# The last edge sum in 16-bit terms: rows of 384 bfloat16 values in place of 128 float32 values

## The reference, cut to what matters

```
h = maximum(layernorm(x), 0.0)
x = x + segment_sum(take(h, dst), src, num_segments=6250)
```

## Time and profile before

| | |
|---|---|
| median of 3 runs | 11695.7 us |
| profiled execution | 11690.42 us |
| its span | 11688.7 us |
| from the end of layer 3's sum to the first gather of `sum_phase` | 9243 to 9330 us |
| gathers of `sum_phase`, 1616 | 9330.3 to 11658.3 us |
| `final_phase` and the stores | 11671.4 to 11688.7 us |

### The profile page before, as it was taken

How to read it: one execution, slowest core, us unless ns; L and a number is a source line. 1 busy time by engine, 2 the same in 40 slices (tenths; PEclk the granted TensorE clock), 3 DMA queues, 4 the chain that set the end, 5 groups by cost and what they waited for, 6 DMA issues and landing times. The chain is left out here.

```text
span 11688.7 us, 111903 instructions
## 1 busy us (share of the span) xinstructions
PE 6256.4 (54%) x29027; PEld 4853.4 (42%) x29027; DVE 6469.5 (55%) x14870; ACT 2647.0 (23%) x8519; POOL 6742.7 (58%) x7099
## 2 busy tenths in 40 slices
PE   8744577777775355555554455555555333333333
PEld 2233455555554333333333455555555333333333
DVE  7799766666664455555554555555555622233223
ACT  0033111111110244444442243444444300000000
POOL 0055566666665566666665455555555466666665
PEclk6555788888887676666666777877777655555555
DMA  0000233333334422222222333333333322222223
GB/s 26 12 10 10 56 76 73 76 76 76 76 75 86 110 46 46 47 47 46 47 46 31 85 85 87 87 87 87 86 87 88 65 46 47 48 47 47 47 47 53
DMA packets 1413627, 706.78 MB, mean 60 GB/s; under 512 B 1170036, under 2 KB 1273944, under 8 KB 1412872
## 3 DMA queue, kind: packets, MB, share of 16 engines
q0 software_dynamic: 254160, 559.07, 19.0%
q1 hardware_dynamic: 1158840, 140.57, 8.6%
HBM read 595.05 MB, written 104.05 MB: 60 GB/s over the span
## 5 line engine op out<-in xcount | busy, mean ns | idle before, releaser
L1042 POOL DMA_INDIRECT l_rows<-h_tab,l_index x1616 | 1525.7, 944 | 942.3 <-issue 452.8
L1425 POOL DMA_INDIRECT l_rows<-h_tab,l_index x1616 | 1527.7, 945 | 868.5 <-issue 472.5
L603 POOL DMA_INDIRECT l_rows<-h_tab,l_words x1616 | 1524.6, 943 | 828.2 <-issue 461.8
L646 PE MATMUL l_sums<-l_onehot,l_rows 128*128 128x128 f32 x3232 | 829.5, 438 | 1599.0 <-issue 875.5
L1560 PE MATMUL l_sums<-l_weighted,l_rows 128*128 128x256 f32 x3232 | 1199.0, 537 | 712.7 <-DVE acc L1487 673.6
L646 PEld LDWEIGHTS l_sums<-l_onehot,l_rows 128*128 128x128 f32 x3232 | 719.6, 328 | 1708.9 <-issue 1076.1
L1947 PE MATMUL l_ps_q<-qtab,h 128*128 x3232 | 831.4, 413 | 1099.6 <-ACT h L1836 783.9
L634 DVE TENSOR_TENSOR acc<-acc,l_sums 128x128 f32 x1616 | 462.6, 286 | 1646.4 <-remote 733.8
L1439 ACT ACTIVATE l_weighted<-l_onehot,l_weights 128x128 f32<-128x128 bf16 x3232 | 987.5, 388 | 1427.2 <-DVE l_onehot L554 1084.1
L1487 DVE TENSOR_TENSOR acc<-acc,l_sums 128x256 f32 x1616 | 677.4, 419 | 1047.8 <-remote 687.4
L759 PE MATMUL src_sums<-tmp 128*128 128x288 f32 x3128 | 1042.2, 486 | 401.8 <-DVE tmp L736 217.7
(11 more groups left out here) (345 smaller groups left out, 11296.6 us busy)
## 6 DMA issues: line engine op xcount, KB each, us to landing
staged<-tmp SPq DMA_DIRECT2D x391, 152.0 KB
l_rows<-h_tab,l_index POOLq DMA_INDIRECT x3232
l_rows<-h_tab,l_words POOLq DMA_INDIRECT x1616
by_src<-words_src SPq DMA_DIRECT2D x96, 152.0 KB
l_kv<-kv_tab,l_words POOLq DMA_INDIRECT x816
l_attr<-in_edge_attr SPq DMA_DIRECT2D x44, 272.0 KB
l_kv<-kv_tab,moments POOLq DMA_INDIRECT x600
h_tab<-h SPq DMA_DIRECT2D x21, 448.0 KB, 3.0
```

What stands on the lines that cost most here:

```text
L603: pool.indirect_dma_start(rows[b][:, j, :], None, table, bass.IndirectOffsetOnAxis(ap=words[k % 3][:, at + j, 0:1], axis=0)).then_inc(rows ...
L646: done = nc.tensor.matmul(sums[q % SUMS][:, j, 0:P], rows[b][:, j, :], onehot[b][:, j, :], start=True, stop=True)
L1042: pool.indirect_dma_start(rows[b][:, j, 0:D], None, table, bass.IndirectOffsetOnAxis(ap=index[q // Q16 % WORDS][:, q % Q16 * H + j, :], ax ...
L1425: pool.indirect_dma_start(rows[b][:, j, :], None, h_tab, bass.IndirectOffsetOnAxis(ap=index[q // Q16 % WORDS][:, q % Q16 * H + j, :], axis ...
```

## The change

The rows of the last table are no longer 128 float32 values but three bfloat16 terms of 128 values each, side by side (768 bytes): the first is h rounded to 16 bits, the second the rounded rest, the third what is left. The one-hot matrices are bfloat16 too.

- `beta_phase`: after the relu of a part, ScalarE rounds h to the first term (`first`), VectorE subtracts it (`rest`), ScalarE rounds the rest to the second term (`second`), and VectorE subtracts again into the third (`third`). SyncE stores the terms of the part, 128 x 7 x 384 x 2 bytes = 672 KB, to `terms_tab`. These steps are interleaved with the other parts' work, a few parts later.
- `sum_phase`: the one-hot is now the loaded matrix, and the row of 384 values the streamed one, in one 16-bit matmul for each tile. Its result is nodes x 384 and fills most of a PSUM bank. There are seven such buffers of one tile in place of three of four tiles. `summed` is raised and waited for at each tile, and each tile's matmul from the eighth on waits for the add of the tile seven before.
- `acc3` is a tile of its own of 128 x 49 x 384 float32, three times the size; each add has 384 columns.
- `final_phase`: no transposes. VectorE adds term 2 and term 3 to term 1, part by part, and then the sum to x: three adds of 128 x 896 values for each of 7 parts, 21 in all. Each add to x waits for the last add of its own part, and the next part's first add stands in between.

```diff
@@ build
-                beta_phase(nc, att, skip, zs, x, h, qtab[:, :, 0:D], moments, stat, eps, of.wz[:], h_tab)
-            sum_phase(nc, "l3", acc3, minus, blk_src, by_src, h_tab)
-            final_phase(nc, acc3, x, ident, out)
+                beta_phase(nc, att, skip, zs, x, h, qtab[:, :, 0:D], moments, stat, eps, of.wz[:], terms_tab)
+        with ExitStack() as last:
+            acc3 = sb("acc3", [P, NB, TERMS * D], F32, last)
+            sum_phase(nc, "l3", acc3, minus, blk_src, by_src, terms_tab)
+            final_phase(nc, acc3, x, out)
@@ sum_phase
-    H, AHEAD, SUMS = G // 2, 2, 3
+    H, AHEAD, SUMS = G // 2, 2, 7
-        rows = [sb(f"rows{b}", [P, H, D]) for b in range(RING)]
-        onehot = [sb(f"onehot{b}", [P, H, P]) for b in range(RING)]
-        sums = [own.enter_context(nc.psum_tensor(f"{tag}_sums{b}", [P, H, GAP], F32)) for b in range(SUMS)]
+        rows = [sb(f"rows{b}", [P, H, TERMS * D], BF16) for b in range(RING)]
+        onehot = [sb(f"onehot{b}", [P, H, P], BF16) for b in range(RING)]
+        sums = [own.enter_context(nc.psum_tensor(f"{tag}_sums{b}", [P, 512], F32)) for b in range(SUMS)]
-        pairs_of = lambda q: 2 * (q + 1)
+        tiles_to = lambda q: H * (q + 1)
-                        pool.wait_ge(summed, pairs_of(q - RING))
+                        pool.wait_ge(summed, tiles_to(q - RING))
@@ sum_phase, vector
-                        if j % 2 == 0:
-                            dve.wait_ge(summed, pairs_of(q - 1) + j // 2 + 1)
-                        if q * H + j > 0:
-                            dve.wait_ge(added, q * H + j)
+                        n = q * H + j
+                        dve.wait_ge(summed, n + 1)
+                        if n > 0:
+                            dve.wait_ge(added, n)
                         a = acc[:, bass.ds(blocks[j], 1), :]
-                        nc.vector.tensor_tensor(a, a, sums[q % SUMS][:, j:j + 1, 0:P], ALU.add).then_inc(added, 1)
+                        nc.vector.tensor_tensor(a, a, sums[n % SUMS][:, 0:TERMS * D].unsqueeze(1), ALU.add).then_inc(added, 1)
@@ sum_phase, tensor
-                        if j % 2 == 0 and q >= SUMS:
-                            pe.wait_ge(added, (q - SUMS) * H + j + 2)
-                        done = nc.tensor.matmul(sums[q % SUMS][:, j, 0:P], rows[b][:, j, :], onehot[b][:, j, :],
-                                                start=True, stop=True)
-                        if j % 2 == 1:
-                            done.then_inc(summed, 1)
+                        n = q * H + j
+                        if n >= SUMS:
+                            pe.wait_ge(added, n - SUMS + 1)
+                        nc.tensor.matmul(sums[n % SUMS][:, 0:TERMS * D], onehot[b][:, j, :], rows[b][:, j, :],
+                                         start=True, stop=True).then_inc(summed, 1)
@@ beta_phase, sync
-                norm_store(sp, h_tab, h, h_ready, h_stored)
+                for r in range(R):
+                    sp.wait_ge(split, r + 1)
+                    sp.dma_start(rows[r], terms[r % 2][:].rearrange("p b n d -> p b (n d)")).then_inc(h_stored, 16)
@@ beta_phase, scalar
+                def first(r):
+                    act.wait_ge(h_ready, r + 1)
+                    if r >= 2:
+                        act.wait_ge(h_stored, 16 * (r - 1))
+                    nc.scalar.activation(terms[r % 2][:, :, 0, :], h[:, part_of(r), :], ACT.Copy).then_inc(rounded, 1)
+                def second(r):
+                    act.wait_ge(rest_ready, r + 1)
+                    nc.scalar.activation(terms[r % 2][:, :, 1, :], tmp[:, part_of(r), :], ACT.Copy).then_inc(rounded2, 1)
@@ beta_phase, vector
+                def rest(r):
+                    dve.wait_ge(rounded, r + 1)
+                    nc.vector.tensor_tensor(tmp[:, part_of(r), :], h[:, part_of(r), :], terms[r % 2][:, :, 0, :], ALU.subtract).then_inc(rest_ready, 1)
+                def third(r):
+                    dve.wait_ge(rounded2, r + 1)
+                    nc.vector.tensor_tensor(terms[r % 2][:, :, 2, :], tmp[:, part_of(r), :], terms[r % 2][:, :, 1, :], ALU.subtract).then_inc(split, 1)
@@ final_phase, vector
+                nc.vector.tensor_tensor(part(0, 0), part(0, 0), part(0, 1), ALU.add).then_inc(added, 1)
+                dve.wait_ge(added, 1)
                 for r in range(R):
                     here = part_of(r)
-                    dve.wait_ge(turned, r + 1)
-                    nc.vector.tensor_tensor(x[:, here, :], x[:, here, :], turns[r % 2][:, 0:LB, :], ALU.add).then_inc(done, 1)
+                    nc.vector.tensor_tensor(part(r, 0), part(r, 0), part(r, 2), ALU.add).then_inc(added, 1)
+                    if r + 1 < R:
+                        nc.vector.tensor_tensor(part(r + 1, 0), part(r + 1, 0), part(r + 1, 1), ALU.add).then_inc(added, 1)
+                    dve.wait_ge(added, 2 * r + 2)
+                    nc.vector.tensor_tensor(x[:, here, :], x[:, here, :], part(r, 0), ALU.add).then_inc(done, 1)
+                    if r + 1 < R:
+                        dve.wait_ge(added, 2 * r + 3)
```

More of the change, by code:

```diff
@@ L577, in sum_phase @@
         rows_ready = [sem(f"rows_ready{b}") for b in range(RING)]
-        oh_ready, summed, added, cleared = sem("onehot_ready"), sem("pair_summed"), sem("added"), sem("cleared")
-        pairs_of = lambda q: 2 * (q + 1)
+        oh_ready, summed, added, cleared = sem("onehot_ready"), sem("tile_summed"), sem("added"), sem("cleared")
+        tiles_to = lambda q: H * (q + 1)
         with nc.Block() as block:
@@ L611, in one_hots @@
                     if q >= RING:
-                        dve.wait_ge(summed, pairs_of(q - RING))
+                        dve.wait_ge(summed, tiles_to(q - RING))
                     if at == 0:
@@ L1973, in beta_phase @@
         att = h
+        terms = [sb(f"terms{n}", [P, LB, TERMS, D], BF16) for n in range(2)]
+        rounded, rest_ready, rounded2, split = sem("rounded"), sem("rest_ready"), sem("rounded2"), sem("split")
         with nc.Block() as block:
@@ L1989, in gate @@
                     nc.scalar.activation(z[:, 1, part_of(r)], z[:, 0, part_of(r)], ACT.Exp).then_inc(e_ready, 1)
-                for r in range(R):
-                    gate(r)
+                def first(r):
+                    act.wait_ge(h_ready, r + 1)
                     if r >= 2:
-                        norm_root(nc, act, stat, eps, r - 2, var_ready, root_ready)
-                    if r >= 3:
-                        norm_relu(nc, act, h, tmp, r - 3, centred, h_ready)
-                for r in range(R - 2, R):
-                    norm_root(nc, act, stat, eps, r, var_ready, root_ready)
-                    norm_relu(nc, act, h, tmp, r - 1, centred, h_ready)
-                norm_relu(nc, act, h, tmp, R - 1, centred, h_ready)
+                        act.wait_ge(h_stored, 16 * (r - 1))
[3 more added lines that the diff above has]
+                    nc.scalar.activation(terms[r % 2][:, :, 1, :], tmp[:, part_of(r), :], ACT.Copy).then_inc(rounded2, 1)
+                for s in range(R + 4):
+                    if s < R:
+                        gate(s)
+                    if 2 <= s < R + 2:
+                        norm_root(nc, act, stat, eps, s - 2, var_ready, root_ready)
+                    if 3 <= s < R + 3:
+                        norm_relu(nc, act, h, tmp, s - 3, centred, h_ready)
+                        first(s - 3)
+                    if s >= 4:
+                        second(s - 4)
             @block.vector
@@ L2027, in _, with final_phase @@
                 ch.link(nc.vector.reciprocal(rden[:], rden[:]))
-                for r in range(R):
-                    attention(r)
-                    if r >= 1:
-                        gate(r - 1)
-                    if r >= 2:
-                        norm_centre(nc, dve, ch, stat, x, tmp, r - 2, root_ready, centred)
-                gate(R - 1)
-                for r in range(R - 2, R):
-                    norm_centre(nc, dve, ch, stat, x, tmp, r, root_ready, centred)
-def final_phase(nc, acc, x, ident, out):
+                def rest(r):
[4 more added lines that the diff above has]
+                    nc.vector.tensor_tensor(terms[r % 2][:, :, 2, :], tmp[:, part_of(r), :], terms[r % 2][:, :, 1, :], ALU.subtract).then_inc(split, 1)
+                for s in range(R + 5):
+                    if s < R:
+                        attention(s)
+                    if 1 <= s < R + 1:
+                        gate(s - 1)
+                    if 2 <= s < R + 2:
+                        norm_centre(nc, dve, ch, stat, x, tmp, s - 2, root_ready, centred)
+                    if 4 <= s < R + 4:
+                        rest(s - 4)
+                    if s >= 5:
+                        third(s - 5)
+def final_phase(nc, acc, x, out):
     R = NB // LB
@@ L2044, in final_phase @@
         sem = lambda name: own.enter_context(nc.semaphore(name))
[L2045 to L2046 removed]
```

(6 more changed lines are left out.)

19 lines of the change are left out of this document (6 added, 13 removed).

## The result

The changed kernel took 11759.5 us (median of 6 runs, 11738.68 to 12039.44) beside 11699.4 us (6 runs, 11684.55 to 11724.0) for the kernel before: ratio 1.0047, 95% interval 1.0032 to 1.0062. It is slower by 55 us, and the forecast was 11780. One of the six runs of the changed kernel, the one of 12039.44, was in a slower state (granted clock 0.633, 0.69 in the others), and the ratio leaves it out. The profiled execution took 11764.2 us with a span of 11762.5, 73.8 us longer than the span of before.

The account below looks back on a forecast made before the run. GpSimd's gather issue, 1.249 us each, plus 313 us of waits for late `summed` notices was taken to bound the last phase. Terms 15 + 0 + 5 + 0 + 53 + 12 = +85 gave 11780 us, 8-in-10 range 11470 to 11950.

Parts of the forecast that it names:

- The term that was said to decide: In `sum_phase`, TensorE may be 7 tiles ahead of the adds, not 12: +53 us, bounds -313 to +312.
- The forecast's own signs for its main term: In `sum_phase`, GpSimd's waits above 0.5 us would total about 370 us, not 325.
- `beta_phase`, predicted +15: 14 subtractions add 15.4 us on VectorE, last relu -1, larger last store +0.6; bounds +8 and +22.
- ScalarE's 14 new copies lie beside it: In `beta_phase`, ScalarE's new copies run beside VectorE's work, adding nothing except at the very end.
- Start of the phase, gathers, TensorE, VectorE: In `sum_phase`: larger memset hidden, 0; 768-byte gathers +5 us; matmuls and 552 ns adds hidden behind 5.0 us a quad, 0.
- far below 801: In `sum_phase`, TensorE's busy time would fall far below 801 in 2250 us, with no gain from it.
- Sums in flight: In `sum_phase`, fewer tiles ahead of the adds, priced by the second phase's pace, 1.475 against 1.442 us: +53 us.
- A: At GpSimd's waits for `summed`, late notices become rarer: half gone -125 us, 11571; all gone -281, 11415; chance 0.26.
- B: Only the ends change; in `sum_phase` seven tiles are as good as twelve, the ring of four quads limits: +32, 11728; chance 0.16.
- C: In `sum_phase`, wider adds and more notices make it much worse: +163 us, 11859, or +344, 12040; chance 0.20.
- Notices for each tile: In `sum_phase`, 1616 notices replace 808; the skill page's 26 ns each gives 21 us, left out of the sum.
- The end, predicted +12: In `final_phase`, 21 adds at 1.06 us, 22.3 us, replace 10.5 us with transposes: +12, bounds +9 and +16.

## Why the prediction was right, and where not

**The forecast.** Slower by 85 us against 73.8 in the profiles, of which 19.6 are drift of unchanged phases; 54 are the change. The direction and the place of the parts that show in every group (`beta_phase` and the end) were right. The term that was said to decide was wrong: first to last gather was to cost 58 us and cost 15.9. That the total came near all the same is luck in good part, since the 15 us missed in `beta_phase` and the 20 us of drift stood in for most of the 42 that did not come. The forecast's own signs for its main term, waits of GpSimd near 370 us, did not come either (339.2, with 341.6 before).

**`beta_phase`, predicted +15, measured +29.8.** The 14 subtractions are there at 1.08 us each, and with three buffers the stretch costs +16.5: that term was sized right. The stretch as measured is above the upper bound of +22. The step that failed is "ScalarE's 14 new copies lie beside it". They do by busy time (33.5 of 117 us), but one of them waits for a store in a queue that VectorE needs. The store of 672 KB lands in 3.5 us, near the 3.6 estimated from the earlier trace rows; its length was counted once, at the end, while its wait came five times.

**Start of the phase, gathers, TensorE, VectorE.** Nearly all as predicted: the memset (15.7 us) is hidden, the gather takes 945 ns against 943 at 512 bytes, the gap stays at 0.30 us, the add is 553 ns against 552 (two chained adds are 0.21 us apart and not 0.145, which is hidden too). The one sign that did not come is TensorE's busy time "far below 801" in 2250 us: it is 761. The work did fall, four matmuls of 384 columns back to back taking 1.44 us where a quad took 2.04 (the estimate was 1.3). But with hold-ups TensorE waits 612.3 us for adds and gets through one tile at a time, and a matmul that stands alone takes 495 ns. Without hold-ups it is busy for 546 us in 1900. As forecast, nothing came of it. In the group without hold-ups the whole phase is 2018.8 us, 1.25 us for each gather.

**Sums in flight, predicted +53, measured nothing.** The step that failed is the use of the second phase's pace as a price for fewer tiles in flight. Eight tiles in place of twelve in the kernel before gave a ratio of 1.0000 (0.9991 to 1.0009), four sums in the changed one 1.0062 against 1.0047 with seven. What then does the phase cost? 11 to 16 us in two pairs of profiles with hold-ups, next to nothing without. Its cause was not taken apart. The adds are a candidate, since leaving out three quarters of them took 59 us off, but whether by their number, their width or their waits no run shows.

**What holds GpSimd.** The prediction rightly put 313 us of the phase on late notices, and rightly said that neither matmul nor add is on the path. It took them as something that can become rarer or more frequent with the way the sums are posted. The runs show something else. Take from each phase the 2019 us of GpSimd's own pace: 308 us stay for before, 324 for the changed kernel, 295 with eight tiles, 321 with twice the ring, 313 with four sums, 262 with a quarter of the adds, and with pauses 345 (342 of it pauses, 134 x (2.68 + 0.17 - 0.30)) and 322 (168 of it pauses). All but one lie between 295 and 345: GpSimd issues no gather for some 13 to 15% of the phase, and a memset can stand in for the waits. Why it is this share the runs do not show, and it is no constant. A quarter of the adds has 11.5%, and the other gather phases of the kernel before have more: set against 1.250, 1.250 and 1.275 us without hold-ups, their paces of 1.523, 1.475 and 1.635 us hold 18, 15 and 22% of standing still, the first two with the same gathers as the last phase (13%). What the other engines do must count as well. That the total hardly moved is why rivals A, B and C were all away from the truth on the phase: A needed the waits to shrink, C to grow, and B had the right amount for the phase (0) from a wrong reason, the ring of four quads, which is no bound (twice the ring, same waits). By the sum, 32 of B plus the 15 of `beta_phase` that it missed would have been 47, near the 54 measured.

**Notices for each tile.** With 1616 notices and without hold-ups the phase is 2018.8 us, the bare pace of GpSimd, so there they cost nothing. The prediction had left the rule of the Trainium skill ("TensorE: Matmul & The Clock Gate", section "The cost: per-tile semaphore tail") out of its sum, and there the runs bear this out. With hold-ups the estimate of 21 us on that page's figure lies near the 11 to 16 measured, and no run tells the notices from other causes. What the Trainium skill says in "Perfetto Trace Analysis" (section "Tensor Engine Instruction (MATMUL, LD_WEIGHTS)") of updates that wait for PSUM's acknowledgement does not explain these hold-ups: with a pause of GpSimd the same matmuls, with the same notices, are followed by adds that wait 4.7 us at most.

**The end, predicted +12, measured +8.8:** 2.3 us less for the last stores, and the adds' pace of 1.01 us where 1.06 was taken.

## What to carry to other kernels

Before you price a change by comparing the paces of two phases, ask what they share. Here GpSimd's issuing and its standing still made up the phase's length: sums in flight and ring depth moved nothing that can be told, and three quarters of the adds only 59 of 2341 us. A new instruction on an engine that is mostly idle still costs when it waits for a transfer and the critical engine's work is queued behind it; give it one buffer more, or put it behind that work. And when a stall survives twice the buffers, put the idle time in yourself: if the total stays, the stall acts as a limit on the rate and not as a latency, and more room will not help.

## What the runs showed of the hardware

- One indirect DMA for 128 rows costs GpSimd 0.944 to 0.949 us (median) and a gap of 0.30, at 512, 768 and 1024 bytes a row; at 1024 bytes single ones are longer, up to 6.6 us, and the mean is 0.975 without hold-ups. The fastest pace seen is 1.25 us for each tile, and 1.275 at 1024 bytes.
- On four of five occasions, gathers issued at this pace without a stop made other engines' steps and notices late (VectorE's step of 57 ns took up to 1425 ns in the changed kernel; in the kernel before the step kept its 57 ns and adds waited up to 9.5 us for a notice). A pause of 2.68 us after every 12 gathers took it away in the one run that has it, one of 1.39 us did not; GpSimd's standstill is about the same in total each way (345 and 322 us). On the fifth occasion there was nothing of it, and the whole program took 9930 us in place of 11552 to 11708. What lies behind it stays open.
- The mean granted clock in the first gather phase's window was 0.99, nearly throughout 2.4 GHz, in the kernel with one wait a quad, where TensorE was busy for 1506 of 1900 us. It was 0.87, a mix of 2.4 and 1.2 GHz, in the changed kernel's first profile, where the hold-ups left it 1660 of 2300. In the last phase it was 0.50, 1.2 GHz, with and without them (busy 761 of 2250 and 546 of 1900 us).
